# Moving ScalarE's scale-and-shift of the later first layers' rows within the slot (split-precision gated graph network)

## What is computed

```python
x = layernorm(x + (adj @ x) @ weight + bias)          # first layer
h = x                                                 # gated layer, 3 steps
for _ in range(3):
    a = adj @ h                                       # a_in and a_out are the same here
    av = concat([a, a])
    z = sigmoid(lin(av, w3) + lin(h, u3))
    r = sigmoid(lin(av, w4) + lin(h, u3))
    hv = tanh(lin(av, w5) + lin(r * h, u5))
    h = (1 - z) * h + z * hv
out = layernorm(x + h)
```

## Time and profile before

| | us |
|---|---|
| median of 3 runs | 1597.66 |
| lowest and highest | 1593.7, 1599.77 |
| the profiled execution | 1599.81 |
| its span, first to last instruction | 1598.0 |
| TensorE busy | 1582.7 (99%) |
| VectorE busy | 1418.2 (89%) |
| ScalarE busy | 1143.2 (72%) |
| GpSimd busy | 304.2 (19%) |
| mean granted TensorE clock | 0.997 |

### The profile page before, as it was taken

The page is one execution under the profiler, slowest core; times in us unless marked ns, Lnnn a source line. Parts: engine busy times, 40 slices in busy tenths (PEclk is TensorE's granted clock), DMA queues, the critical chain, the costliest instruction groups (busy, mean ns, idle before and its releaser), DMA issues.

```text
span 1598.0 us, 21623 instructions
## 1 busy us (share of the span) xinstructions
PE 1582.7 (99%) x7114; PEld 1310.6 (82%) x7114; DVE 1418.2 (89%) x1512; ACT 1143.2 (72%) x2306; POOL 304.2 (19%) x392
## 2 busy tenths in 40 slices
PE   9999999999999999999999999999999999999997
PEld 8888888888888788888888888888888888888885
DVE  7988888998899898898989998999989999888888
ACT  5677667777776777777686776867777777776666
POOL 5111111121111221212212112111122111210013
PEclk9999999999999999999999999999999999999998
DMA  5555556676567765677757776576765776556444
GB/s 193 178 178 179 192 166 202 222 242 214 178 220 217 231 217 170 216 233 223 229 165 221 228 241 207 172 223 220 238 203 189 220 235 214 170 157 198 168 149 158
DMA packets 232898, 322.67 MB, mean 202 GB/s; under 512 B 23121, under 2 KB 198098, under 8 KB 232786
## 3 DMA queue, kind: packets, MB, share of 16 engines
q1 hardware_dynamic: 232368, 320.96, 63.6%
q10 hardware_dynamic: 418, 0.33, 0.1%
HBM read 162.34 MB, written 158.86 MB: 201 GB/s over the span
## 4 chain that ended last, share of the span: by engine, by line
PE 74%; DMA 10%; SPq 6%; DVE 4%; ACT 2%; issue 2%; POOL 1%; DVEq 0%; ACTq 0%; POOLq 0%
PE ps_r L486 37%; PE ps_h L486 25%; PE ps_a L595 6%; SPq L329 5%; DMA h_scratch_b<-h_blocks_b 4%; PE ps_l L543 3%; PE ps_l L562 2%; DMA h_scratch_a<-h_blocks_a 1%; DMA a_landed<-a_scratch_a 1%; DMA a_landed<-a_scratch_b 1%; DMA xw_scratch<-h_blocks 1%; DMA a_scratch_a<-a_blocks 1%; DVE a_blocks L1149 1%; PE ps_l L552 1%; DVE h_blocks L1050 1%
## 5 line engine op out<-in xcount | busy, mean ns | idle before, releaser
L716 ACT ACTIVATE rh_hi<-rh 128x512 fp32r<-128x512 f32 x192 | 118.7, 633 | 200.7 <-DVE rh L1177 200.7
L1149 DVE STREAM_TRANSPOSE a_blocks<-ps_a 128x1024 f32<-128x1024 f32 x92 | 113.8, 1236 | 74.0 <-PE ps_a L595 74.0
L887 ACT ACTIVATE rh<-ps_r,bias_r 128x512 f32<-128x512 f32 x192 | 126.1, 682 | 47.6 <-PE ps_r L486 43.3
L899 ACT ACTIVATE z_sb<-ps_r,bias_z 128x512 f32<-128x512 f32 x192 | 122.6, 678 | 14.6 <-PE ps_r L486 14.4
L996 DVE TENSOR_TENSOR rh_lo<-rh,rh_hi 128x512 fp32r<-128x512 f32 x192 | 124.7, 689 | 9.4
L1189 DVE TENSOR_TENSOR hv<-hv,z_sb 128x1024 f32<-128x1024 f32 x95 | 121.1, 1275 | 9.9
L903 ACT ACTIVATE hv<-ps_h,bias_h 128x512 f32<-128x512 f32 x192 | 121.4, 678 | 11.0 <-PE ps_h L486 11.0
L486 PE MATMUL ps_r<-h_hi,u_hi 128*128 128x512 f32 x384 | 119.0, 391 | 1.0 <-ACT z_sb L899 1.0
L486 PE MATMUL ps_r<-a_hi_a,w_hi 128*128 128x512 f32 x384 | 118.7, 390 | 1.2 <-ACT rh L887 1.2
L486 PE MATMUL ps_h<-rh_hi,u_hi 128*128 128x512 f32 x384 | 119.4, 391 | 0.0
L486 PE MATMUL ps_r<-a_hi_b,w_hi 128*128 128x512 f32 x384 | 118.6, 390 | 0.6 <-ACT rh L887 0.5
(11 more groups left out here) (408 smaller groups left out, 4129.3 us busy)
## 6 DMA issues: line engine op xcount, KB each, us to landing
h_scratch_a<-h_blocks_a SPq DMA_DIRECT2D x48, 512.0 KB, 4.3
h_landed_a<-h_scratch_a SPq DMA_DIRECT2D x192, 128.0 KB, 2.9
h_scratch_b<-h_blocks_b SPq DMA_DIRECT2D x47, 512.0 KB, 4.1
h_landed_b<-h_scratch_b SPq DMA_DIRECT2D x188, 128.0 KB, 2.9
a_scratch_a<-a_blocks SPq DMA_DIRECT2D x46, 512.0 KB, 2.7
a_landed<-a_scratch_a SPq DMA_DIRECT2D x184, 128.0 KB, 3.2
a_scratch_b<-a_blocks SPq DMA_DIRECT2D x46, 512.0 KB, 2.7
a_landed<-a_scratch_b SPq DMA_DIRECT2D x184, 128.0 KB, 3.2
```

The source lines that it names most:

```text
L716: return act.activation(dst, src, ACT.Copy)
L887: act.activation(rh[:, c, :], ps_r[:, c, :], ACT.Sigmoid, bias=bias_r[:, c:c + 1]).then_inc(r_ready, 1)
L899: act.activation(z_sb[:, c, :], ps_r[:, c, :], ACT.Sigmoid, bias=bias_z[:, c:c + 1]).then_inc(z_ready, 1)
L1149: tr = dve.transpose(flat_blocks(a_blocks).rearrange("p (x e) -> p x e", e=Q), flat(ps_a).rearrange("p (x f) -> p x f", f=Q))
```

## The change

ScalarE's `first_norm(g)` for the groups 8 to 31 (`BY_FEATURE`) is issued behind `reset_gate(s)` and `reset_high(s)` of the same slot, ahead of `graph_high(s + 1)`; before, it was issued right behind `candidate(s - 1, 1)`, ahead of `node_high(s + 2)` and `state_high(s + 1)`. The groups 4 to 7 stay where they were. Instructions, waits, semaphores and buffers are the same.

```diff
                 if 1 <= s <= SLOTS:
                     candidate(s - 1, 1)
-                if (g := group_at(s, NORM)) is not None:
+                if (g := group_at(s, NORM)) is not None and g not in BY_FEATURE:
                     first_norm(g)
...
                 if s < SLOTS:
                     reset_gate(s)
                     reset_high(s)
+
+                if (g := group_at(s, NORM)) in BY_FEATURE:
+                    first_norm(g)
                 if s == 1:
                     state_high(s + 1)
                 if s + 1 < SLOTS:
                     graph_high(s + 1)
```

## The result

| | before | after |
|---|---|---|
| median, us (runs) | 1598.72 (1593.7 to 1601.57, 6) | 1609.2 (1607.01 to 1611.13, 6) |
| profiled execution, us (span) | 1599.81 (1598.0) | 1608.95 (1607.2) |

The ratio is 1.0069, with an interval of 1.005 to 1.0088: the change costs 10.5 us by the two medians. The forecast was 1598.9 us and its range ended at 1604. The time lies on the side of rival (b) and beyond its price of 1605.5.

The account below looks back on a forecast made before the run. TensorE was taken as the bound, with at most 6.5 us to gain outside it. Terms -1.47 + 2.3 + 0.4 = +1.2 us on the median 1597.66 gave 1598.9 us, range 1594 to 1604.

Parts of the forecast that it names:

- rival (b): Slower: VectorE's delay goes through SyncE in full, at the read `a_landed` behind `a_blocks`; about 1605.5 us, chance 0.12.
- What bounds the kernel: TensorE is the bound; its lost time, read from matmul starts over slots 4 to 94, is some 6.5 us.
- The gain at the front: Reset-gate waits in slots 33, 36 and 69 go, 1.65 us, less 0.18 for `rh_hi`: gain 1.47 us.
- The update gate in norm slots: In eleven of 24 slots with the moved step, late `z_sb` delays the next state product 0.21 us: loss 2.3 us.
- What it costs further down: `ax_lo` and `a_blocks` come 2.0 us late; SyncE passes some 0.95 to slot 28's update gate: loss 0.4 us.
- The clock: Added waits could return TensorE to 1.2 GHz, a slot then taking some 15 us more; chance 0.01.

Follow-up runs that it names:

- e5_gates_first: The changed kernel with the two update gates ahead of `a_hi` in norm slots (those with the moved step): 1611.4 us, ratio 1.0074.
- e13_vector_1us_end: The kernel before with three unused statistics instructions (1.0 us) on VectorE behind `h_blocks` in each norm slot: 1610.77 us, ratio 1.0079.
- e6_blocks_first: The changed kernel with VectorE's transpose `h_blocks` ahead of `ax_lo` in norm slots: 1603.91 us, ratio 1.0036.
- e3_late_bias: The changed kernel with GpSimd's first bias addition held back until the state is finished, like the second: 1606.41 us, ratio 1.0055.
- e14: The kernel before with six unused statistics instructions (2.0 us) on VectorE behind `h_blocks` in each norm slot: 1627.61 us, ratio 1.0186.
- e16_shifted: The kernel before with only an unused tensor of 72 bytes per partition allocated ahead of `h_t`, no instruction added: 1639.86 us, ratio 1.0258.

## Why the prediction was wrong

**What bounds the kernel: right.** Reading lost time from starts of matmuls held, and all of the loss is found there.

**The gain at the front: right in place and size.** Slots 33, 36 and 69 fell from 15.51 to 15.07, 14.96 and 14.96, 1.54 us against 1.65 less 0.18. The reset gate's lateness fell from 3.2 to 1.2 us in all; that of slot 30 went too, which I had not taken, but slot 30 then waited 0.22 + 0.375 + 0.11 us for `rh_hi` and 0.91 at its end for the update gate. Of the 1.2 us that are left 1.06 are new, in slot 51, where ScalarE had waited for the landing `h_landed_b`. One reading was off: the four w3 waits of the earlier trace rows are those of slots 30, 33, 36 and 69; slot 57 is a fifth that the list doesn't hold.

**The update gate in norm slots: the mechanism right, the size too small.** TensorE is late by 4.8 us, 1.3 before: a rise of 3.5 against 11 x 0.21 = 2.3. Of the eleven slots that I had named nine are late by 0.17 to 0.21 us, as worked out; 42 and 51 are late by 0.31 and 0.99. And four of the thirteen for which I had taken nothing are late too: 21, 30, 33 and 57, by 0.21 to 0.91. In all four `a_hi` starts 0.29 to 0.60 us behind the end of the step (slot 30: at 539.35, 0.60 behind), so its landing was last. Before, `a_hi` had waited for that landing longer than the step lasts, and I took this as room that stays. That the landings come later by VectorE's delay, through SyncE, is my reading, as landings move between executions too. Slots 30 and 57 had been late by 0.57 each before. e5_gates_first shows that taking these waits away, at the price of a later `a_hi`, doesn't bring the time down.

**"What it costs further down", 0.4 us: the step that failed.** In its place the runs show 5.2 us more of waits for `rh_hi` in norm slots and 1.6 more for the update gate in the slots behind. The first half is right: `ax_lo` was forecast near 293.57 and `a_blocks` near 295.87, and they came at 293.81 and 296.11, in a trace whose slot 15 starts 0.28 us later. From there I asked one question, whether SyncE passes the delay on, and took the slack of one slot for each. Four things were wrong.
- I wrote of VectorE's idle stretches that they "still suffice". They lie at the start of norm slots only (0 to 2.8 us, none in slots 33 and 69), and the delay of 2 us arises right behind a norm slot. VectorE has no idle time ahead of `a_blocks` in the next two slots (0 and 1.0 us in sum over all of them before), so what is left of the delay is carried for two slots (on average 1.2 and 0.9 us) and eats the stretch of the next norm slot: 34.3 to 15.5 us.
- I called the reset multiply of the next slot early by 0.3 us and stopped. Nowhere did I ask what GpSimd does meanwhile. The row that shows the collision stood in the trace of before: 1.81 us for an operation that elsewhere takes 1.18. What counts is when the engines meet: in slot 18 the addition now falls wholly onto one operation of 1.22 us and costs 1.1 us in place of 0.6.
- So TensorE lost 0.5 to 0.7 us on `rh_hi` in ten norm slots, +5.2 us, the largest part of the loss. I had no term for this.
- The one loss that I had written, 0.36 us at the end of slot 28, did not come. SyncE passed on nearly the whole delay there, not half: `a_landed` is issued 8.35 us behind the slot's start, before 6.51. But it landed 1.4 us sooner after that, `a_hi` was 0.44 us later, and the update gate ended 0.27 us ahead of the state product. Slots 58, 64, 67 and 70 lost instead, 0.3 to 0.9 us each, all with `a_hi` waiting for its landing; of these slot 58 had lost 0.7 before.

e13_vector_1us_end shows this chain with ScalarE untouched and e6_blocks_first, by time, that cutting it at its start gives half of the loss back. e3_late_bias cuts it in the middle: the waits for `rh_hi` go, the time hardly falls. The links between are read from the traces of slots 15 to 18. What stays open is how much of the 10.5 us is the collision alone: when e3 took it away, other waits took most of it up, so the shares can't be told apart by taking one away.

**Rival (b)** had the right sign and named VectorE's delay, but said it goes through SyncE to the update gate. That way took a part (some of the 3.5 us more in norm slots, and the 1.6 us more behind them); the way through the reset product took more. Its chance of 0.12 was too small, because I weighed the delay only where I had a path for it. Its sum takes back 0.5 us of gain where the forecast has 1.47, without a reason.

**The clock: right.** The windows shown are at a granted 1.00, the level of 2.4 GHz, and the mean over the whole of e14, with waits of up to 1.6 us, is 0.997, as before.

## What to carry over

When a step moves on an engine with slack, look at each engine that waits for it, and ask of a nearly full one not how busy it is on average but how many slots lie between the delay and its next idle stretch: here 1 us of VectorE's time, taken in 24 slots, cost half a microsecond of the kernel each time. An operation that is longer in some slots than in others (1.81 against 1.18 us) marks a collision whose price changes when either engine shifts; list these before calling a delay hidden. An engine's idle time in front of a waiting instruction is well filled with work that it has anyway: with the step one place earlier, which alone brought the change from +10.5 to -1.1 us, two such fills brought it to -5.4. And a relief that works alone can cost time beside another, so measure them together.

## What the runs showed of the hardware

**VectorE and GpSimd take turns.** A two-operand operation of VectorE on 128x1024 elements takes 1.18 to 1.23 us by itself, and 2.28 to 2.35 when GpSimd's addition on 128x512 starts with it; beside it GpSimd's operations on 128x4 go from 0.20 to 1.25. The Trainium skill ("GPSIMD Engine Reference", section "Specifications") says that the two share their SBUF interfaces and contend when VectorE reads two SBUF inputs. The traces agree, and show the size: for whole instructions, not a slowdown in proportion. They also show the other side: VectorE's transpose, with one input, and the addition both keep their times when they run together (1.25 at 333.37 and 1.30 at 333.41 after).

**72 bytes of allocation per partition cost 41.6 us.** In e16_shifted the pairs lie 0.46 to 0.47 us apart, where the same pairs before lie 0.45 apart; over a slot the matmul takes 0.2333 in place of 0.2267 us, in slots that wait for nothing and at a granted clock of 1.00. Which operand's address it is, and why, no run shows.

**A short wait has a second price.** Behind each such wait of TensorE the next matmul but one is 0.11 us late. Where the second of two copies is awaited too, 0.375 us come on top, which are no price of the wait but a wait themselves: the second copy ends 0.60 us behind the first, and the matmuls are spaced by 0.2267. So the 0.22 us by which the first `rh_hi` was late in slot 18 went with a loss of 0.70.
